# Loads and stores of the second pass issued by one engine instead of two

## The reference

```python
PARTITIONS = _partitions()          # the 15 set partitions of (i0, i1, o0, o1)
...
def _basis_apply(X, W, blocks, eye_n, ones_n):
    ...
    return jnp.einsum(expr, *ops) / denom
```

## Time and profile before

| | |
|---|---|
| median of 3 runs | 1950.24 us |
| lowest, highest | 1950.18, 1955.7 us |
| span of the profiled execution (first to last instruction) | 1947.9 us |
| TensorE, VectorE busy | 81%, 67% of the span |
| moved by DMA | 821.81 MB, 422 GB/s over the span |

### The profile page before, as it was taken

The page is one execution under the profiler, slowest core; times in us unless marked ns, Lnnn a source line. Parts: engine busy times, 40 slices in busy tenths (PEclk is TensorE's granted clock), DMA queues, the critical chain, the costliest instruction groups (busy, mean ns, idle before and its releaser), DMA issues.

```text
span 1947.9 us, 42202 instructions
## 1 busy us (share of the span) xinstructions
PE 1573.7 (81%) x19274; PEld 965.8 (50%) x19278; DVE 1297.6 (67%) x1260; ACT 81.8 (4%) x85; POOL 295.6 (15%) x670
## 2 busy tenths in 40 slices
PE   6888888888888899997777777777787787777785
PEld 5877888887888853443333333333333333333332
DVE  5988889888988846775555555555555555555554
ACT  0111110011111110000000000000000000000000
POOL 7433444333333310000000000000000000000000
PEclk9999999999999998999999999999999999999998
DMA  9999999999999979999999999999999999999998
GB/s 379 415 413 415 425 428 429 429 427 429 429 427 430 427 316 384 429 429 430 432 431 431 430 431 431 430 430 432 431 430 431 431 432 431 430 431 431 431 430 370
DMA packets 58796, 821.81 MB, mean 422 GB/s; under 512 B 8376, under 2 KB 8504, under 8 KB 9080
## 3 DMA queue, kind: packets, MB, share of 16 engines
q1 hardware_dynamic: 39048, 551.77, 66.8%
q10 hardware_dynamic: 19696, 269.40, 32.4%
HBM read 551.75 MB, written 269.09 MB: 421 GB/s over the span
## 4 chain that ended last, share of the span: by engine, by line
DMA 74%; PE 15%; DVE 6%; issue 4%; SPq 0%; ACT 0%; DVEq 0%
DMA early<-strip_in 28%; DMA early<-pairs 25%; DMA out<-early 21%; PE ps L881 11%; DVE ring_own L618 3%; PE ps L758 2%; DVE early L728 1%; DVE early L736 1%; PE ps L783 0%; PE ps L889 0%; PE ps L888 0%; PE ps L862 0%; PE ps L809 0%; PE ps L769 0%; ACT early L583 0%
## 5 line engine op out<-in xcount | busy, mean ns | idle before, releaser
L881 PE MATMUL ps<-ring_own,mixer 128*128 128x512 f32 x1252 | 593.0, 631 | 140.7 <-DMA ring_own<-strip_in 114.1
L758 PE MATMUL ps<-early 128*64 128x66 f32 x16896 | 554.9, 225 | 123.8 <-DMA early<-pairs 112.0
L618 DVE TENSOR_REDUCE ring_own<-early 128x32 f32<-128x2048 f32 x264 | 590.6, 2281 | 79.6 <-DMA early<-pairs 79.5
L758 PEld LDWEIGHTS ps<-early 128*64 128x64 f32 x16896 | 537.4, 139 | 141.1 <-DMA early<-pairs 96.0
L728 DVE SCALAR_TENSOR_TENSOR ring_own<-ps,row_sum,stage 128x512 f32<-128x512 f32 (+3 forms) x233 | 301.6, 1295 | 322.0 <-PE ps L881 322.0
L881 PEld LDWEIGHTS ps<-ring_own,mixer 128*128 128x128 f32 x1252 | 246.8, 202 | 487.2 <-issue 471.9
L881 PE MATMUL ps<-early,mixer 128*128 128x512 f32 x800 | 376.5, 627 | 89.6 <-DMA early<-strip_in 81.6
L728 DVE SCALAR_TENSOR_TENSOR early<-ps,row_sum,stage 128x1024 f32<-128x1024 f32 (+2 forms) x152 | 192.5, 1267 | 199.1 <-PE ps L881 199.1
L881 PEld LDWEIGHTS ps<-early,mixer 128*128 128x128 f32 x800 | 157.0, 201 | 308.7 <-issue 294.9
L443 POOL TENSOR_TENSOR gram_all<-gram_all,stage 128x512 f32<-128x512 f32 x132 | 167.6, 1291 | 0.0
L736 DVE SCALAR_TENSOR_TENSOR ring_own<-ps,row_sum,stage 128x488 f32<-128x488 f32 (+43 forms) x308 | 133.4, 475 | 0.0
(11 more groups left out here) (137 smaller groups left out, 101.9 us busy)
## 6 DMA issues: line engine op xcount, KB each, us to landing
early<-pairs SPq DMA_DIRECT2D x132, 2080.0 KB, 15.3
ring_own<-strip_in SPq DMA_DIRECT2D x78, 2048.0 KB, 49.1
out<-ring_own ACTq DMA_DIRECT2D x78, 2048.0 KB, 38.5
early<-strip_in SPq DMA_DIRECT2D x50, 2048.0 KB, 49.0
out<-early ACTq DMA_DIRECT2D x50, 2048.0 KB, 38.5
const<-const_f SPq DMA_DIRECT2D x1, 773.5 KB, 23.7
ring_own<-dia_pair SPq DMA_DIRECT2D x1, 640.0 KB, 23.5
ring_own<-half_in SPq DMA_DIRECT2D x1, 512.0 KB, 34.5
```

What stands on the lines that cost most here:

```text
L618: nc.vector.tensor_reduce(part_sum[:, t % sums], pairs_of(s), AX.XYZ, ALU.add).then_inc(summed, 1)
L758: last = mm(regions(parity)[lane:lane + WIDE, m // BANK_REGIONS, m % BANK_REGIONS], chunk(slot, k, False), chunk(slot, k, True), start=ope ...
L881: last = mm(ps[:, first + at // BANK, 0:piece], mixer[:, :, :].rearrange("p a m -> p (a m)"), buf[:, at:at + piece], start=True, stop=True)
```

## The change

SyncE issues the stores too. It now walks over the units u = 0 to 128; for each it waits until the unit is finished, issues its store, and then issues the loads that have become possible. A load is possible when the unit that had its slot before is at least LAG = 2 places back, and SyncE waits for that unit's store to land before it issues the load. The loads keep their order. The first load into slot 9 (L13) isn't issued before S8. ScalarE issues only `out_dia` in the second pass.

```diff
+        LAG = 2
...
-            for u in range(own_twos + 1 + reuse, len(units)):
-                _, s, turn = home(u)
-                if turn == 0 and s >= own_twos + reuse:
-                    sp.wait_ge(col_term_done, banks)
-                    sp.wait_ge(row_term_done, 1)
-                    sp.wait_ge(dia_ready, 1)
-                if turn:
-                    sp.wait_ge(z_out[s], 16 * turn)
-                load(u)
+            coming = list(range(own_twos + 1 + reuse, len(units)))
+            strips_before = list(itertools.accumulate(len(unit) for unit in units))
+            slots = [home(u)[1] for u in range(len(units))]
+            for u in range(len(units)):
+                buf, s, _ = home(u)
+                sp.wait_ge(finished, strips_before[u])
+                sp.dma_start(half_out if s == TWOS else twos_out[units[u][0] // 2], buf).then_inc(z_out[s], 16)
+                while coming:
+                    _, s, turn = home(coming[0])
+                    if turn == 0:
+                        if u < 8:
+                            break
+                        sp.wait_ge(col_term_done, banks)
+                        sp.wait_ge(row_term_done, 1)
+                        sp.wait_ge(dia_ready, 1)
+                    else:
+                        if max(w for w in range(coming[0]) if slots[w] == s) > u - LAG:
+                            break
+                        sp.wait_ge(z_out[s], 16 * turn)
+                    load(coming.pop(0))
...
             for p, (u, k, q) in enumerate(order):
-                buf, s, _ = home(u)
-                if k == len(units[u]) - 1:
-                    act.wait_ge(finished, p + 1)
-                    act.dma_start(half_out if s == TWOS else twos_out[units[u][0] // 2], buf).then_inc(z_out[s], 16)
```

## The result

The changed kernel takes 1960.25 us (median of 6 runs, 1958.6 to 1963.96) against 1950.8 us for the kernel before in the same comparison (6 runs, 1948.59 to 1955.7). The ratio is 1.0039, 95% interval [1.0025, 1.0053]: slower by 9.5 us, 0.4%. I had said 1961.0 us.

What follows compares the result with a forecast made beforehand. DMA was taken to bound the kernel, without slack in the second pass. Idle DMA at its start, 12.3 - 1.5 = 10.8 us, other terms 0, gave 1950.24 + 10.8 = 1961.0 us; range 1958 to 1964, wider 1954 to 1975.

Steps and rivals of the forecast that it cites:

- The start of the pass: Start of the second pass: late loads leave DMA idle 12.3 us against 1.5 before, a loss of 10.8 us.
- The second way, by bytes: Check of the start-up loss: 3.6 MB fewer moved by 794.3 us, 8.4 us, taken as the lower end.
- The times of the stores: Second pass start: `finished` sets the same store times in both kernels, S0 at 731.75 us to S8 at 794.3.
- the gaps: Idle DMA at the second pass's start: 2.0 us before S1, S2, S6, S7 and S8 each, 2.3 before S5.
- Unit 13: SyncE waits for S13 before issuing L20 to L23; queued work covers this with some 9 us left.
- Steady state: Rest of the second pass: LAG costs nothing, 0 us; four transfers, 19.5 us, stay queued behind the awaited store.
- Turns: Changes between loads and stores in one queue: taken as 0 us; rival that they cost something, chance 0.15.
- The rival of cheaper whole transfers: Whole transfers in one direction pass better than packets of two queues in turn, making the kernel faster; chance 0.07.
- The drained queue: Rival: the queue empties at each wait for a landed store, 116 us per idle microsecond per pair; chance 0.03.
- the 1.5 us of a lone store: Time a lone store takes beyond its data, used as upper bound for a change of direction.
- The two rules of the Trainium skill: A fixed 2 us per transfer, not counted, and separate issuing engines for inputs and outputs, which speaks against this change.
- The end: Last loads and stores of the second pass: DMA full in both kernels, 0 us.

Runs made afterwards that it cites:

- run 2: Changed kernel (one queue) with the loads at the start placed where two queues had them, L10 behind S0 to L13 and L14 behind S4: 1952.16 us, ratio 1.0001.
- run 3: Kernel before (two queues) with only the changed kernel's start-up delay, L10 to L16 held until units 2, 3, 4 and 8 are finished: 1962.44 us, ratio 1.0062.
- Run 1: Changed kernel with one number different, 8 to 4, so L13 may go out behind S4 instead of S8: 1955.32 us, ratio 1.0014.
- run 5: Changed kernel with LAG = 1 instead of 2; L10 goes out behind S1, L13 still behind S8: 1959.53 us, ratio 1.0052.
- runs 7 and 8: Changed kernel with second-pass loads and stores split in two 1 MB transfers: 1974.54 us; then also ordered store, load, store, load from unit 16 on: 1976.38 us.
- run 6: Changed kernel issuing two stores then two loads in turn from unit 16 on, half as many changes of direction: 1966.8 us, ratio 1.0075.
- run 4: Changed kernel with LAG = 0 instead of 2, each load waiting for the store issued just before it: 2371.62 us, ratio 1.2133.
- run 9: Changed kernel with LAG = 0, SyncE also waiting from unit 16 on for each load before the store, every transfer alone: 2450.75 us, ratio 1.2546.

## Why the prediction was right, point by point

- **The start of the pass, 10.8 us.** Right in place and in cause: the late loads. Runs 2 and 3 show it from both sides. The total is right too: 9.5 us by the medians, 10.0 by the spans, 10.6 by the missing bytes. But it came out so by luck in part, because the terms inside it were off both ways. I had counted 12.3 us of idle DMA against 1.5 before. The shares give (1 - 0.85) x 62.6 = 9.4 us against 0.03 x 62.6 = 1.9, so 7.5 us more and not 10.8. The 2.3 us before S5 did not come:

```profile
771.40:773.70 2.30, 2.30 (x7) 1.00 (x6) 2.05 (x3) 0.00 (x0) 0.00 (x0) 1.00 1.00 429
```

The queued work, slower from 747 to 760 us, lasted past S5. So from 772 to 794 us DMA was idle for 0.16 x 22 = 3.5 us, where the prediction expected to see 8. What I had not on the list is DMA that is busy and slow, and it filled the sum up. The second way, by bytes, was exact as far as it went: 3.6 MB were expected to be missing at 794.3 us, and 3.6 MB were, 8.3 us. Of these 7.5 are the idle time and 0.8 are slower work. The slow refilling after 794.3 us adds 1.0 MB, 2.3 us, and that makes the 10.6. What makes a refilling queue slow, no run isolates.
- **The times of the stores.** S0 was issued at 733.16 us and not at 731.75. The coefficients were ready 1.4 us later in this execution: from 700 to 704 us the granted clock of TensorE was 0.57, in the kernel before 1.00, which is 1.7 us of work. S5 came at 773.47 and not at 773.71, so from there on the program kept the times that were worked out.
- **Which edit does it.** I had priced the gaps one by one: two before S1 and S2, four before S5 to S8. Run 1 left 3.0 us where the gaps of 2.0 + 2.0 - 1.5 = 2.5 us should be left. In the changed kernel itself the number 8 in the condition on L13 sets the loss: run 5 moves L10 to L12 forward and gains nothing. Once L13 is early, the places of L10 and L11 count too: run 2, which moves them as well, has none of the 3.0 us left. Their difference, 3.2 us, is no more than the intervals leave open (3 us to each side).
- **Unit 13.** L19 was issued at 826.94 us (825 expected), and L20 at 862.94 (858.6 expected). SyncE waited 4 us longer than worked out, yet the queue did not run dry: 429 GB/s in the window from 856 to 867 us.
- **Steady state, 0 us.** Right. From L26 at 897.01 to L128 at 1893.83 us there are 102 intervals of 9.773 us; before, 9.767. Landing after 24.4 us was expected as 24.4 plus about 1, and 28.9 as 29.3 plus about 1.
- **Turns, 0 us.** Right, by runs 7 and 8 (0.002 us each) and by run 2, where the 232 turns cost at most 3 us together, 0.013 us each, if nothing else gave that back. The rival of cheaper whole transfers has no support either: run 6 made the runs in one direction longer and got no faster pace.
- **The drained queue.** At LAG = 2 the depth covers it, at LAG = 1 too, at LAG = 0 it costs 411 us. The bound that I used for a queue that runs empty, the 1.5 us of a lone store, was too small for a load by half (2.9 us). It stood only as the end of a range and did not touch the sum.
- **The two rules of the Trainium skill.** The Trainium skill (DMA: Bandwidth & Descriptors, "Anatomy of one DMA") gives its 2 us beside a transfer's bytes for transfers that GpSimd issues, and the prediction left that out. Here SyncE and ScalarE issue them: the 2 us lie between the 1.5 us and the 2.9 us of lone transfers, and do not hold in a filled queue, where halving the transfers cost 0.06 us for each additional one. By the Trainium skill (Perfetto Trace Analysis, "DMA Optimizations"), it may make sense to have one issuing engine for inputs and another for outputs. That gave nothing by itself here: run 2 equals the kernel before within 3 us. What it protects from is the mistake that was made here, a load that stands behind stores for no reason.
- **The end, 0 us.** Right. The last store was issued at 1929.95 us and landed 27.3 us later, and from 1936 to 1942 us, with stores alone, 434 GB/s were moved.

## What to carry to other kernels

In this kernel, whose second pass is full of DMA, the order of the transfers was free as long as the queue stayed filled, and each gap was paid for in full, with the slow refilling on top. So look for the places where it isn't filled, which are the start of a pass and wherever a condition on one buffer holds back those queued behind it. When you add up idle time, work out the loss by bytes as well: nothing can have been moved that was not yet issued. Merging two queues into one program order makes each issue wait for everything written ahead of it: write each load where its buffer comes free at the start, not by the rule of the steady state. Two transfers of 2 MB behind the one that is awaited were depth enough here (run 5); with none behind it the kernel took a fifth longer (run 4).

## What the runs showed of the hardware that I had not expected

- A lone load of 2 MB takes 7.8 us and a lone store of the same size 6.3 us (run 9), though both move at 4.9 us each in a filled queue.
- A queue that restarts is slow while it is busy: 312 GB/s at a DMA share of 0.84 with LAG = 0, 414 GB/s at 1.00 after 794 us in the changed kernel, 417 at 1.00 there with two queues (run 3). The share of busy time alone understates such a loss; GB/s shows it.
- Changing direction cost 0.002 us in a filled queue (runs 7 and 8), no more than can be told from nothing. Cutting the same bytes into twice the transfers cost 0.06 us for each additional one, with packets of 7.3 KB in place of 14.6 KB.
- The granted clock of TensorE can decide a difference between two kernels whose DMA is full: 0.50 and not 1.00 from 720 to 728 us, ahead of the second pass, made run 6 about 4 us longer.
